# Gathers, statistics and output bias of the third attention layer rearranged, with idle products ahead of the experts

## The reference

```python
def _layernorm(x, axis=-1, eps=1e-05):
    m = jnp.mean(x, axis=axis, keepdims=True)
    v = jnp.var(x, axis=axis, keepdims=True)
    return (x - m) / jnp.sqrt(v + eps)
...
# experts: two of eight for each row, weighed by gates
    out = eo[e_id, p_id]
    out = jnp.where(token_mask[..., None].astype(bool), out, x[..., None, :])
    return jnp.einsum('btkd,btk->btd', out, gates)
...
# third layer's attention
        scores = jnp.einsum('bhsd,bhtd->bhst', qh, kh) / jnp.sqrt(jnp.float32(D_K))
        attn = jax.nn.softmax(scores, axis=-1)
        out = jnp.einsum('bhst,bhtd->bhsd', attn, vh)
        out = out.transpose(0, 2, 1, 3).reshape(B, -1, H * D_K)
        return out @ W_o + b_o
...
    x = x + jnp.tanh(g_ffn[1]) * _L1_ffn_ref(_layernorm(x, axis=-1), ...)
    x = x + jnp.tanh(g_xattn[2]) * _L2_xattn_ref(_layernorm(x, axis=-1), ctx_1024, ctx_1024, ...)
    x = x + jnp.tanh(g_ffn[2]) * _L2_ffn_ref(_layernorm(x, axis=-1), ...)
```

## Time and profile before

| | |
|---|---|
| median of 3 runs | 1183.06 us (1182.45 to 1183.79) |
| profiled execution | 1181.22 us, its span 1179.4 |
| mean granted clock | 0.882 |
| TensorE products busy | 930.3 us, 79% of the span |
| VectorE busy | 921.9 us, 78% |
| ScalarE busy | 694.3 us, 59% |
| GpSimd busy | 503.0 us, 43% |

### The profile page before, as it was taken

The page is one execution under the profiler, slowest core; times in us unless marked ns, Lnnn a source line. Parts: engine busy times, 40 slices in busy tenths (PEclk is TensorE's granted clock), DMA queues, the critical chain, the costliest instruction groups (busy, mean ns, idle before and its releaser), DMA issues.

```text
span 1179.4 us, 29916 instructions
## 1 busy us (share of the span) xinstructions
PE 930.3 (79%) x11473; PEld 725.2 (61%) x11491; DVE 921.9 (78%) x2227; ACT 694.3 (59%) x1807; POOL 503.0 (43%) x614
## 2 busy tenths in 40 slices
PE   4999989989999940999699999677799996333332
PEld 3888869978887830566378878233488885112221
DVE  3888876857899871566489998689577786999997
ACT  3887864347777720445377777556487875445542
POOL 4344411233357766232499994355523331221222
PEclk9999998999999965899899999789999998565555
DMA  7830000000000012465111110000000000000000
GB/s 204 256 128 3 3 2 2 2 1 2 2 14 27 29 41 74 123 180 148 44 34 29 29 32 9 1 1 1 1 2 3 2 2 2 5 14 13 14 10 18
DMA packets 60526, 44.42 MB, mean 38 GB/s; under 512 B 15196, under 2 KB 55781, under 8 KB 59366
## 3 DMA queue, kind: packets, MB, share of 16 engines
q1 hardware_dynamic: 54996, 33.96, 9.7%
q0 software_dynamic: 4096, 8.34, 2.3%
q10 hardware_dynamic: 1298, 0.27, 0.1%
HBM read 23.73 MB, written 18.87 MB: 36 GB/s over the span
## 4 chain that ended last, share of the span: by engine, by line
PE 54%; DVE 27%; issue 8%; POOL 6%; ACT 2%; DVEq 2%; DMA 1%; ACTq 0%; POOLq 0%; another core or an unknown queue 0%
PE ps L585 8%; PE ps L518 8%; PE ps L547 6%; PE ps L609 4%; PE ps L592 3%; PE ps L570 3%; PE ps L565 3%; DVE rowmax L1411 3%; DVE sm L1416 3%; PE ps L646 2%; PE ps L655 2%; PE ps L647 2%; POOL big L950 2%; PE ps L557 2%; DVE q_b L1641 2%
## 5 line engine op out<-in xcount | busy, mean ns | idle before, releaser
L1411 DVE TENSOR_REDUCE rowmax<-ps 128x16 f32<-128x1024 f32 x128 | 156.1, 1219 | 77.1 <-PE ps L547 76.8
L773 ACT ACTIVATE pr<-ps 128x512 f32<-128x512 f32 x256 | 153.2, 601 | 17.0 <-PE ps L518 15.7
L1416 DVE TENSOR_TENSOR sm<-ps,rowmax 128x1024 f32<-128x1024 f32 x128 | 156.6, 1223 | 3.4
L585 PE MATMUL ps<-vbd,pr 128*64 128x18 f32 x4096 | 146.8, 214 | 2.2 <-ACT pr L773 2.2
L518 PE MATMUL ps<-cst,sm 128*128 128x128 f32 x1024 | 138.5, 279 | 11.5 <-DVE sm L1416 11.1
L585 PEld LDWEIGHTS ps<-vbd,pr 128*64 128x64 f32 x4096 | 134.3, 139 | 15.3 <-ACT pr L773 2.8
L1004 POOL TENSOR_SCALAR xn<-x_sb,mv_all,rstd_all 128x128 f32<-128x128 f32 x128 | 102.6, 801 | 82.5 <-PE ps L524 79.9
L803 ACT ACTIVATE vbd<-ps 64x128 f32<-64x128 f32 x256 | 71.4, 279 | 100.5 <-PE ps L571 94.8
L518 PEld LDWEIGHTS ps<-cst,sm 128*128 128x128 f32 x1024 | 112.2, 141 | 19.1 <-DVE sm L1416 16.8
L807 ACT ACTIVATE qbd<-ps,bqp,cst 128x128 f32<-128x128 f32 x256 | 105.3, 467 | 6.9 <-PE ps L571 3.7
L1079 POOL TENSOR_TENSOR q_out<-q_b,q_s 128x1280 bf16<-128x1280 bf16 (+2 forms) x18 | 38.2, 2120 | 137.5 <-DVE q_b L1642 137.5
(11 more groups left out here) (244 smaller groups left out, 2363.9 us busy)
## 6 DMA issues: line engine op xcount, KB each, us to landing
slots<-hT SPq DMA_DIRECT2D x8, 1024.0 KB, 10.9
sm<-slots SPq DMA_DIRECT2D x32, 256.0 KB, 3.1
expert_out<-xn_all SPq DMA_DIRECT2D x16, 256.0 KB, 2.8
ew<-in_L_ffn_w SPq DMA_DIRECT2D x24, 128.0 KB, 2.5
out<-x_sb SPq DMA_DIRECT2D x32, 64.0 KB, 1.5
slots<-xn_all,row_s POOLq DMA_INDIRECT x64
big<-expert_out,row_g POOLq DMA_INDIRECT x64
x_sb<-in_x SPq DMA_DIRECT2D x1, 512.0 KB, 6.6
```

Source lines behind the costliest of these rows:

```text
L585: last = nc.tensor.matmul(dst[:, :, h2, :], probs[:, h2, :], heads[:, :, h2, :], start=True, stop=True, skip_group_check=True)
L773: nc.scalar.activation(pr[y][:, b, :], bank(y, b), ACT.Exp, scale=SCALE).then_inc(p_ready[y], 1)
L1411: v.tensor_reduce(row3, sc, AX.X, ALU.max).then_inc(rowmax_ready[x], 1)
L1416: v.tensor_tensor(sm[x][:, :].rearrange("p (r g k) -> p r g k", r=RG, k=S), sc, row3.unsqueeze(3).broadcast_to([P, RG, 4, S]), ALU.subtrac ...
```

## The change

In the third layer two tiles (four gathers) are fetched ahead of the stage and tile t + 4 within it; two tiles are mixed ahead and tile t + 2 within, from t = 0 on, in the buffers of its own s. GpSimd has a function of its own for this layer, mixed_rows: up to t = 0 power and xn come before the two gathers, from t = 1 behind them, and the power of four columns for the next stage stands between the gathers. The addition of y_bias_b on GpSimd and VectorE's wait for it are gone; instead TensorE adds the bias behind L592 as a product of a row of ones by y_bias[2], into the same place. TensorE does 26 idle products ahead of the experts, once GpSimd has come to the scatters of tile 30 (scatters_late), and 18 instead of 22 ahead of the third layer, without waiting for a mean.

```diff
--- before.py
+++ after.py
@@ -55,7 +55,7 @@
 
 
         for t in range(-2, T + 3):
-            half(t, t % NS, *((t + d) // NS if 0 <= t + d < T and (t >= 0 or d != 3) else None for d in (6, 3, 2, 1, 0, -1, -2, -3)))
+            half(t, t % NS, *((t + d) // NS if 0 <= t + d < T else None for d in (4, 2, 2, 1, 0, -1, -2, -3)))
 
     def routed(t):
 
@@ -320,7 +320,7 @@
         mix_step, early_bst, early_aggr, early_eps, early_rstd = (sems(n) for n in (
             "mix_step", "early_bst", "early_aggr", "early_eps", "early_rstd"))
         got_in = [sems(f"got_in{p}_") for p in range(2)]
-        out_done = sem("out_done")
+        out_done, scatters_late = sem("out_done"), sem("scatters_late")
 
         block = stack.enter_context(nc.Block())
 
@@ -589,7 +589,10 @@
                         count_batch(t, y)
                     if old is not None:
                         pe.wait_ge(oT_ready[x], IT * l + old + 1)
-                        nc.tensor.matmul(bank(y, 3)[:, 2 * P:3 * P], oT[x][:, :], wo[l][:, :], start=True, stop=True).then_inc(y_ready[x], 1)
+                        last = nc.tensor.matmul(bank(y, 3)[:, 2 * P:3 * P], oT[x][:, :], wo[l][:, :], start=True, stop=(l != 2))
+                        if l == 2:
+                            last = nc.tensor.matmul(bank(y, 3)[:, 2 * P:3 * P], one_row, y_bias[2][:, :], start=False, stop=True)
+                        last.then_inc(y_ready[x], 1)
                     if l >= 2 and t <= 0:
                         keep_clock(5)
 
@@ -656,6 +659,8 @@
                                                     ew[p][:, 2, c * P:(c + 1) * P], start=(c == 0), stop=(c == 1))
                     last.then_inc(eo_psum[s], 1)
 
+            pe.wait_ge(scatters_late, 1)
+            keep_clock(26)
             for s in range(NS):
                 turn_slots(0, s, False)
             with pe.Fori(0, E // 2 - 1) as j:
@@ -674,8 +679,7 @@
                     last = nc.tensor.transpose(bank_b(1, 2 + n % 2)[:, c * P:(c + 1) * P], w_q[:, n, c * P:(c + 1) * P], ident_b[:, :])
                 last.then_inc(wt_psum, 1)
             pe.wait_ge(wt_ready, 5)
-            pe.wait_ge(early_eps[0], EARLY + 1)
-            keep_clock(22)
+            keep_clock(18)
 
             attention(2)
 
@@ -975,15 +979,44 @@
                     return None
                 return next(b for b, (first, end) in enumerate(BATCHES) if first <= u < end), u
 
+            def mixed_rows(t, x, fetch, later, new, prev, oldest):
+                k, y = ATTENTION_STAGE[2], 1 - x
+
+                def rows():
+                    if later is not None:
+                        u = later * NS + x
+                        mixed_rstd(x, later)
+                        if new is not None:
+                            pool.wait_ge(xnT_psum[x], IT * k + new + 1)
+                        pool.wait_ge(early_rstd[x], EARLY + later + 1)
+                        nc.gpsimd.tensor_scalar(xn[x][:, :], x_sb[:, u * D:(u + 1) * D], mv_all[:, 2 * u:2 * u + 1], rstd_all[:, u:u + 1],
+                                                ALU.subtract, ALU.mult).then_inc(xn_ready[x], 1)
+
+                if t <= 0:
+                    rows()
+                if fetch is not None:
+                    if prev is not None:
+                        pool.wait_ge(sm_ready[y], IT * 2 + prev + 1)
+                    gather(x, fetch, 0)
+                if t > 3 and four_measured(2, (t - 4) // NS):
+                    rstd_of(k, (t - 4) // NS, x, 4)
+                if fetch is not None:
+                    if new is not None:
+                        pool.wait_ge(s_psum[x], IT * 2 + new + 1)
+                    gather(x, fetch, 1)
+                if t > 0:
+                    rows()
+                if t == T + 2:
+                    rstd_of(k, IT - 1, y, 4)
+
             def attention(l):
                 k = ATTENTION_STAGE[l]
 
                 def half(t, x, fetch, further, later, ahead, new, prev, old, oldest):
                     y = 1 - x
-                    if l == 2 and fetch is not None:
-                        if prev is not None:
-                            pool.wait_ge(sm_ready[y], IT * l + prev + 1)
-                        gather(x, fetch, 0)
+                    if l == 2:
+                        mixed_rows(t, x, fetch, later, new, prev, oldest)
+                        return
                     if l == 1 and scattered(t) is not None:
                         if prev is not None:
                             pool.wait_ge(sm_ready[y], IT * l + prev + 1)
@@ -995,8 +1028,6 @@
                             pool.wait_ge(pool_prep, RSTD_FIRST)
                         elif k == 0:
                             pool.wait_ge(early_rstd[x], (u - FIRST) // NS + 1)
-                        elif l == 2:
-                            pool.wait_ge(early_rstd[x], EARLY + later + 1)
                         else:
                             pool.wait_ge(rstd_ready[x], IT * (k - 1) + later + 1)
                         if new is not None:
@@ -1004,10 +1035,6 @@
                         nc.gpsimd.tensor_scalar(xn[x][:, :], xt, mv_all[:, 2 * u:2 * u + 1], rstd_all[:, u:u + 1], ALU.subtract, ALU.mult).then_inc(xn_ready[x], 1)
                         if l == 0 and u == 0:
                             pool.wait_ge(dve_prep, FIRST_Y_BIAS)
-                    if l == 2 and fetch is not None:
-                        if new is not None:
-                            pool.wait_ge(s_psum[x], IT * l + new + 1)
-                        gather(x, fetch, 1)
                     if l == 1 and scattered(t) is not None:
                         if new is not None:
                             pool.wait_ge(s_psum[x], IT * l + new + 1)
@@ -1021,8 +1048,6 @@
                             pool.wait_ge(w0_in, 48)
                             nc.gpsimd.tensor_copy(w_rawf[:, :, :, :].rearrange("p n c d -> p (n c d)"),
                                                   w_raw[:, :, :, :].rearrange("p n c d -> p (n c d)")).then_inc(pool_prep, 1)
-                    if l == 2 and further is not None:
-                        mixed_rstd(y, further)
                     if oldest is not None and l == 1:
                         rstd(k, oldest, y)
                     if oldest is not None and four_measured(l, oldest):
@@ -1047,6 +1072,8 @@
 
             for b, (first, end) in enumerate(BATCHES):
                 for u in range(max(first, scattered(T + 2)[1] + 1), end):
+                    if u == T - 2:
+                        pool.sem_inc(scatters_late, 1)
                     for c in range(2):
                         scatter(b, u, c)
             with pool.Fori(0, E) as e:
@@ -1057,13 +1084,9 @@
             for p in range(2):
                 for s in range(NS):
                     pool.wait_ge(eo_stored[p][s], 16 * E // 2)
-            for i in range(2):
-                for s in range(NS):
-                    for k in range(2):
-                        gather(s, i, k)
             for s in range(NS):
-                mixed_rstd(s, 0)
-            mixed_rstd(0, 1)
+                for k in range(2):
+                    gather(s, 0, k)
             attention(2)
 
             def over_blocks(k, c, x, h, width, src, factor, op):
@@ -1247,7 +1270,7 @@
 
             def mixed_eps(s, i):
                 dve.wait_ge(early_aggr[s], EARLY + i + 1)
-                v.tensor_tensor(mv_all[:, bass.ds(2 * (i * NS + s), 2)], mv[1 - s][:, :], eps2, ALU.add).then_inc(early_eps[s], 1)
+                v.tensor_tensor(mv_all[:, bass.ds(2 * (i * NS + s), 2)], mv[s][:, :], eps2, ALU.add).then_inc(early_eps[s], 1)
 
             def statistics(k, i, s):
                 moments(after_stage(k, i, s))
@@ -1346,7 +1369,7 @@
 
                 def half(t, x, fetch, further, later, ahead, new, prev, old, oldest):
                     y = 1 - x
-                    mixes = l == 2 and further is not None
+                    mixes = l == 2 and further is not None and t >= 0
                     measures = oldest is not None
                     first = measured_first(t) if l == 0 else None
                     if old is not None:
@@ -1357,7 +1380,8 @@
                         dve.wait_ge(o_psum[x], n)
                         v.reciprocal(rden[x][:, :], o3[:, :, HD]).then_inc(rden_ready[x], 1)
                     if oldest is not None:
-                        dve.wait_ge(x_biased[y], IT * l + oldest + 1)
+                        if l != 2:
+                            dve.wait_ge(x_biased[y], IT * min(l, 2) + oldest + 1)
                         residual(k, oldest, y, tg[:, l:l + 1], x, 2 * P)
                     if l == 0:
                         take_weights(t, x)
@@ -1372,12 +1396,12 @@
                         dve.wait_ge(second_in if first < SECOND else rest_in, 32)
                         v.bn_stats(bst[x][:, :], x_sb[:, first * D:(first + 1) * D]).then_inc(early_bst[x], 1)
                     if mixes:
-                        mix(y, further, 0)
```

(25 more changed lines are left out.)

## The result

The kernel after took 1207.69 us (median of 4 runs, 1195.48 to 1216.32) against 1183.19: a ratio of 1.0145, 95% interval 1.0092 to 1.0199. A second set of runs of the same kernel gave 1197.22 against 1182.83, 1.0112 (1.0060 to 1.0164). The ratios leave out the runs marked slow, here 1216.32 and 1215.93, so the first is smaller than the quotient of its two medians. Slower, as forecast, but by 13 to 17 us by the ratios (14 and 24 by the medians), where 5.1 were forecast, and outside the range of 1179.5 to 1191.5. The times of one kernel scatter here by 10 us and more, those of the kernel before too (1181.39 to 1195.16 beside the second set).

A forecast was written before the change was run, and what follows sets the result against it. It took TensorE, busy nearly throughout at full clock, as the bound, with GpSimd costing little. Terms -4.9 + 9.1 + 0.9 + 0 = +5.1 us gave 1186.3 for the profiled execution, 1188.2 against the median; range 1179.5 to 1191.5.

The forecast's parts named there:

- The start: Start of the third layer: first row maximum 6.6 us sooner, third near 596.4 against 601.34; worth -4.9 us (-3.5 to -6.6).
- Product of one row: End of each third-layer half on TensorE: two tile-shape changes, 0.42 us in and 0.36 out, making TensorE's half 4.93 us.
- tile changes are free: Rival for the bias product: shape changes cost nothing, half 4.61 us, -4.3 us in all, time 1178.8; chance 0.13.
- Statistics moved on GpSimd: covered by 0.6: Third-layer halves: xn waits for the same half's mean, but power and xn end 0.6 us before TensorE wants xn.
- the forecast that they would go: Third layer: row maxima would stand 4.9 us apart, without the long halves of the kernel before.
- Idle products: Ahead of the experts: 0 us, between 0 and -2.6; ahead of the third layer: cost nothing, slower ones up to 1 us.
- Behind the layer: Behind the last row maximum: two more one-row products without cover, 0.42 to 0.48 us each, +0.9 us.
- Halves 2 to 30: The third layer's 29 halves after the first: 4.93 us each instead of 4.615, +9.1 us in sum.

The follow-up runs named there:

- e_full_again: The kernel after with its bias product made of two full 128x128 tiles instead of one row; ratio to the kernel before 1.0086.
- e_product_only: The kernel before with one edit, the third layer's output bias as a one-row product on TensorE instead of GpSimd's addition; ratio to the kernel before 1.0116.
- e_start_two: The kernel before with a new third-layer start (four gathers, two mixed tiles ahead), tile t + 5 gathered in half t, GpSimd still adding the bias; ratio 1.0079.
- e_two_twin: e_start_two run once more, on another chip; ratio to the kernel before 1.0077.

## Why the prediction was wrong

- **The start: right in its gain, short by its cost.** First row maximum 12.8 behind the first gather instead of 19.4, 6.6 us sooner as worked out. The third came 24.0 behind it, in the second profile 24.3, against 28.4 before: 4.4 and 4.1 sooner, where 4.9 were forecast.
- **Product of one row: mechanism right, size 0.05 short.** Way in 0.42 as in the earlier trace rows, way out 0.41 where I had taken 0.36: TensorE takes 4.98 and sets the half, 1.4 us more in the layer than with 4.93. That the row maxima stand 4.91 apart in many halves, as forecast, is chance: it is the length of GpSimd's ring, which I had not seen. The sum took the other engines' limit for 4.615, the half of before. In the new order the ring takes 4.87 to 4.95 on three of the four chips that ran it; with no product at all halves of 4.90 and 4.87 were measured on two of them. There the product costs at most 0.1 us a half, and the rival "tile changes are free", priced at 1178.8, would have had a half of 4.88 (e_full_again) and not 4.61.
- **"Statistics moved on GpSimd: covered by 0.6": the step that failed.** It holds in a plain half, where TensorE doesn't wait for xn. But with xn made of a mean of the same half nothing lies in store, and one standstill of GpSimd of 2.52 us is more than the 0.6: TensorE waits 1.55 us for xn, and its clock, a term that the step put at nothing, is at half for 10.2 us behind that. 6.73 + 8.69 less two halves of 4.93 are 5.6 us, and 5.6 again in the second profile; with the order of before e_product_only loses 1.6 at this place. I had weighed the clock ahead of the experts only. Why GpSimd stands still, and why the clock falls in some executions and not in others after such a pause (in e_full_again TensorE waits 1.62 us at this place and its clock stays at 1.00), is open.
- **The same step overlooked where GpSimd's work falls.** It counted the work (4.0 in 4.93). The gather moved from +2.1 to between +0.5 and +1.2 behind the transposes of sm, onto the end of the scores, and the row maxima are tied to it. Behind TensorE's 4.98 this costs little in the kernel after; it is what leaves no gain when the product is taken out. The long halves of the earlier trace rows were read as the length of the powers alone, where up to 0.4 us of each is a tied row maximum; and the forecast that they would go failed, since halves with a power of four still take 5.2.
- **Idle products: right**, about 0 in both places, though they ran 15 us before the place that I had read from the code.
- **Behind the layer: right in this profile**, +0.9; +1.5 in the second.

Halves 2 to 30 add up: 142.97 forecast, 5.6 for the two long halves, and 1.6 because the other 27 average 4.99 instead of 4.93 (1.4 of it TensorE's 4.98), together 150.1 against 150.13 measured.

The profiled execution was 21.2 us slower: 9.4 up to the end of the second layer, 1.0 less from there to the first gather, 6.7 less from the gather to the first row maximum, 18.6 in the third layer and 0.9 behind it. The 9.4 are no effect of the change, as far as the runs show: the second layer took 159.1 in the second set, and the first or second layer lost 6 to 10 us in six of the eighteen other profiles of changed kernels. The 1.0 is not there in the second profile either.

## What to carry to other kernels

Removing a part of a change and seeing the loss stay doesn't clear that part: two limits of nearly the same height (4.98 and 4.88 here) hide each other, and one size that fits is no proof of the cause. Before moving work on an engine with slack, mark at which offset in the period each of its long instructions starts, and look in the trace of before for periods in which it already started there: the long halves showed what the new place costs. And work done ahead of a dense stage is also a store against standstills; what eats it exposes every pause, and behind a pause of TensorE of 1.55 us two halves here ran at half clock for 10 us in all.

## What the runs showed of the hardware

- A row maximum that waits for TensorE starts 1.27 to 1.44 us behind the start of an indirect gather on GpSimd that overlaps the end of the scores, ScalarE's copy 0.03 later; on one of five chips it doesn't. Whether the signal is held, or what else ties them, is not shown.
- A semaphore increment in GpSimd's stream ran about 15 us, eleven or twelve indirect transfers, ahead of the transfer behind it, in all ten profiles that have it.
- GpSimd stands still for 1.5 to 2.6 us about 16 gathers ahead of the last, in sixteen of the nineteen profiles of changed kernels; in the one profile of the kernel before no such gap is seen.
- Changing from a tile of 128x128 to one of 1x128 and back costs 0.35 us (halves of 4.98 and 4.63 on chip 5).
- The same code settles into halves of 4.95 or of 4.50, and can change from one to the other within a layer (e_start_two, e_two_twin).
